# One layer of delta-rule attention and a routed feed-forward: two small TensorE products change places with the projections beside them

## The reference, cut to what matters

```python
q = l2norm(silu(conv4(xn @ Wq)))      # xn = layernorm(x), k alike, v without l2norm
k = l2norm(silu(conv4(xn @ Wk)))
v = silu(conv4(xn @ Wv)); beta = sigmoid(xn @ Wb)
for each token:                       # per head, S is 64 x 64
    u = beta * (v - k @ S)
    S = S + outer(k, u)
    o = q @ S
x = x + rmsnorm(o) * norm_w @ Wo
x = x + ffn(layernorm(x))
```

## Time and profile before

| what | value |
|---|---|
| three runs | 1350.03, 1355.93, 1358.77 us, median 1355.93 |
| span of the profiled execution | 1354.5 us; its own time is not listed beside it |
| mean granted TensorE clock of that execution | 0.984 |
| PE busy over the span | 1305.2 us |
| DVE, ACT, POOL busy | 868.2, 372.6, 336.6 us |

### The profile page before, as it was taken

The page is one execution under the profiler, slowest core; times in us unless marked ns, Lnnn a source line. Parts: engine busy times, 40 slices in busy tenths (PEclk is TensorE's granted clock), DMA queues, the critical chain, the costliest instruction groups (busy, mean ns, idle before and its releaser), DMA issues.

```text
span 1354.5 us, 27271 instructions
## 1 busy us (share of the span) xinstructions
PE 1305.2 (96%) x8466; PEld 824.9 (61%) x8467; DVE 868.2 (64%) x2426; ACT 372.6 (28%) x816; POOL 336.6 (25%) x396
## 2 busy tenths in 40 slices
PE   8968999999999999999999999999999999999996
PEld 7857777887777556544444455555555555555553
DVE  4896688559667523845111477777777777777774
ACT  4745545555453223220000011111111111111111
POOL 1211214232222211313564012212222122122221
PEclk9989999999999999999999999999999999999997
DMA  4525742733456496246447555566665565664420
GB/s 158 97 45 112 109 111 68 147 96 82 98 132 156 103 238 136 81 148 219 190 179 249 174 123 109 110 173 149 134 140 130 128 138 128 129 135 74 73 50 1
DMA packets 208513, 171.05 MB, mean 126 GB/s; under 512 B 71472, under 2 KB 160560, under 8 KB 208432
## 3 DMA queue, kind: packets, MB, share of 16 engines
q1 hardware_dynamic: 135056, 114.16, 32.3%
q0 software_dynamic: 16496, 34.23, 12.8%
q10 hardware_dynamic: 56880, 21.54, 7.6%
HBM read 91.06 MB, written 82.73 MB: 128 GB/s over the span
## 4 chain that ended last, share of the span: by engine, by line
PE 53%; DVE 2%; issue 0%; POOLq 0%; DVEq 0%; ACT 0%
PE pD L2182 15%; PE pG L2162 14%; PE pU L2171 13%; PE pG L2126 3%; PE pU L2126 3%; PE pD L2145 3%; DVE ups L2072 1%; PE pU L2120 1%; PE pD L2140 0%; POOLq L1897 0%; DVE w L1784 0%; DVE w L1785 0%; DVE route_keep L1783 0%; DVE q L1803 0%; DVE qf L1796 0%
## 5 line engine op out<-in xcount | busy, mean ns | idle before, releaser
L2072 DVE STREAM_TRANSPOSE ups<-a 32x96 f32<-32x96 f32 (+1 forms) x1264 | 330.2, 261 | 42.9
L1969 POOL DMA_INDIRECT out<-y,ix x79 | 123.0, 1557 | 482.0 <-ACT y L2025 328.3
L2182 PE MATMUL pD<-w,ups 128*128 (+1 forms) x474 | 219.3, 599 | 3.6 <-DVE ups L2072 3.6
L2171 PE MATMUL pU<-w,xsT 128*128 x632 | 199.9, 459 | 0.0
L2162 PE MATMUL pG<-w,xsT 128*128 x632 | 199.9, 458 | 0.0
L2162 PEld LDWEIGHTS pG<-w,xsT 128*128 128x128 f32 x632 | 119.5, 189 | 88.4 <-issue 37.5
L2171 PEld LDWEIGHTS pU<-w,xsT 128*128 128x128 f32 x632 | 120.1, 190 | 66.9
L950 PE MATMUL pProj<-front_region 128*128 128x256 f32 x624 | 158.4, 398 | 2.0 <-ACT front_region L697 1.6
L2182 PEld LDWEIGHTS pD<-w,ups 128*128 128x128 f32 (+1 forms) x474 | 90.8, 192 | 98.0 <-issue 81.7
L1311 DVE SCALAR_TENSOR_TENSOR front_region<-front_region,cw 128x256 f32<-128x256 f32 x288 | 131.7, 498 | 14.5 <-ACT front_region L733 11.1
L950 PEld LDWEIGHTS pProj<-front_region 128*128 128x128 f32 x624 | 115.3, 194 | 21.5 <-ACT front_region L733 2.3
(11 more groups left out here) (240 smaller groups left out, 1591.8 us busy)
## 6 DMA issues: line engine op xcount, KB each, us to landing
w<-in_up_T SPq DMA_DIRECT2D x16, 1408.0 KB
slot_rows<-zeros SPq DMA_DIRECT2D x79, 266.0 KB, 6.5
xs<-slot_rows ACTq DMA_DIRECT2D x316, 64.0 KB
w<-in_down_T SPq DMA_DIRECT2D x16, 512.0 KB
front_region<-in_L_attn_hidden_states SPq DMA_DIRECT2D x16, 256.0 KB, 3.8
x2r<-in_L_attn_hidden_states SPq DMA_DIRECT2D x16, 256.0 KB, 5.0
partial_sums<-x2r SPq DMA_DIRECT2D x16, 256.0 KB, 3.6
x_normed<-x2n SPq DMA_DIRECT2D x16, 256.0 KB, 2.4
```

The lines of the kernel that those rows point to most:

```text
L1969: pool.indirect_dma_start(out=flat, out_offset=bass.IndirectOffsetOnAxis(ap=ix[1 - par][:, 0:1], axis=0), in_=y[1 - par][:, :], in_offset= ...
L2072: dve.transpose(aT[par][B * to:B * to + B, 0:n, rows], a[rows, 0:len(IC) * P].rearrange("p (c n) -> p c n", c=len(IC))[:, 0:n, B * to:B * ...
L2171: mm = pe.matmul(pU[0][:, 0:I], xsT[par][:, k, :], w[:, bass.ds(slot, 1), 2 * I * k + I:2 * I * (k + 1)], start=(k == 0), stop=(k == DC - 1))
L2182: mm = pe.matmul(pYq[:, :], aT[1 - par][0:m, c, :], down[0:m, :, UPW + D * c:UPW + D * (c + 1)], start=(c == 0), stop=(c == 2))
```

## The change

Three moves, no instruction added or taken away. On PE, `merge_x(u)` goes from behind the slot 0 projection to directly behind `hop_r`, and `scores(u + 1)` goes from ahead of the slot 1 projection to behind it, directly ahead of `hop_u`. On ACT, `x_copy(u)` goes from behind the slot 0 `raw_copy` to ahead of it.

```diff
@@ ACT, slot loop @@
                     if tile_ok(u) and s in (2, 5):
                         s_copy(u, s // 3)
                         o_copy(u, s // 3)
+                    if s == 0 and tile_ok(u) and u < FUSED:
+                        x_copy(u)
                     if even and pair_ok(pk):
                         raw_copy(3 * DC * pk + s)
...
                     if tile_ok(u) and s in (1, 4):
                         u_copy(u, s // 3)
-                    if tile_ok(u) and s == 0 and u < FUSED:
-                        x_copy(u)
@@ PE, slot loop @@
                     if tile_ok(u) and s in (2, 5):
                         hop_o(u, s // 3)
-                    if s == 1 and tile_ok(u + 1):
-                        scores(u + 1)
+                    if s == 0 and tile_ok(u):
+                        merge_x(u)
                     if even and pair_ok(pk):
                         project(3 * DC * pk + s)
                     if not even and pair_ok(pq) and not (pq == PAIRS - 1 and s >= 4):
                         project(3 * DC * pq + SLOTS + s)
                     if old == PAIRS - 1 and even and s < 2:
                         project(3 * DC * old + SLOTS + 4 + s)
+                    if s == 1 and tile_ok(u + 1):
+                        scores(u + 1)
                     if tile_ok(u) and s in (1, 4):
                         hop_u(u, s // 3)
...
                     if s == 0:
-                        if tile_ok(u):
-                            merge_x(u)
                         if u + 3 == NT - 2:
                             qT(NT - 1)
```

## The result

The changed kernel takes 1357.98 us, the kernel before 1354.34 us (medians of 20 runs each): a ratio of 1.0028 with a 95% interval of 1.0014 to 1.0041. That is 3.6 us more, small but resolved. The forecast was +4.1 us, and 1360 us in all, which is 2.0 too high; 1.6 of that comes from the starting point, a median of three runs at 1355.93.

What follows compares the result with a forecast made beforehand. PE, busy 1305.2 of 1354.5 us, was taken as the bound. Terms 1 to 3 gave 5.7 us, the clock -1.6, so +4.1 to a span of 1358.6, and with 1.4 for the median 1360 us, range 1355 to 1365.

Steps and rivals of the forecast that it cites:

- Term 1: Tiles 0 to 10: merge_x loses the projection hiding its wait on ACT's copy, and waits 0.32 to 1.06 us.
- Term 2: Slots 0 and 1: second projection starts 1.00 us after the first, waiting for ACT's bank reads, in odd tiles and 10.
- Term 3: Tiles 0 to 10: fewer changes between large and small products on PE save 0.20 us a tile.
- Absorption: Tiles 3 and 7, where DVE carries the inverse: PE's delay of 0.56 us is taken back, leaving 0.
- Term 4: Even tiles with betas: one stretch of low clock fewer, -1.6 us, bounds -4.9 and +3.3.
- slower rival: New waits around merge_x lower the clock in 11 tiles: 1374.6 us, half of it, 1366, likelier; chance 0.16.
- faster rival: Clock stays up in all even tiles and the first copy is ready in time: 1353 or 1349 us; chance 0.17.

Runs made afterwards that it cites:

- e3: Changed kernel with ACT's copy of the first merge product (w_copy) ahead of the two silus of slot 5: ratio 0.9961 to the kernel before, six runs.
- e6: Changed kernel without zero_rows in tiles 0 and 1, those stores being made later: ratio 1.0022 to the kernel before.
- e9: Changed kernel with w_copy ahead of the silus and zero_rows kept out of tiles 0 and 1: ratio 0.9989 to the kernel before.
- e11: The kernel of e3 run once more: ratio 0.9989 to the kernel before, median 1352.07 us.
- e5: Changed kernel, but tile 1 keeps the old place of merge_x on PE and x_copy on ACT: ratio 1.0005 to the kernel before.
- e8: The kernel before, unchanged, run for a second profile: one time of 1352.28 us.
- e10: The kernel before with zero_rows kept out of tiles 0 and 1, as control: ratio 0.9996 to the kernel before.
- e2: The kernel before with only the scores moved, directly ahead of hop_u: ratio 0.9985 to the kernel before.
- e1: Changed kernel with scores back at the old place, so only merge_x and x_copy moved: ratio 1.0006 to the kernel before.
- e4: Changed kernel with ACT's x_copy back behind raw_copy: ratio 1.0031 to the kernel before.
- e7: Changed kernel with w_copy ahead of the silus and tile 1 in the old order: ratio 0.9980 to the kernel before.

## Why the prediction was right, point by point

- **Term 1** (merge_x loses its cover, 5.9 us over 11 tiles) held: 6.5 us in 12 waits, of which tile 11 had 0.7 already. Tiles 5, 6 and 10 came to 0.34, 0.94 and 1.06 us between the end of hop_r and merge_x, against 0.35, 0.93 and 1.06. Tile 8 was off, 0.93 instead of 0.33: PE was late in tile 7 (half clock in its output product, shown above), so merge_w had no DMA wait, and ACT lost the head start that this wait had given it. The output product of tile 7 is at half clock in seven of the thirteen profiles, of both orders, and exactly those seven have no DMA wait in tile 8. That the queue of ACT is the cause is shown by e3: the waits fell to 1.3 us. The Trainium skill states the rule ("TensorE: Matmul & The Clock Gate", section "Architectural detail: the array is 16× 32×32, not 1× 128×128": ScalarE works strictly in order), and e3's 5.2 us agree with it.
- **Term 2** (projections wait for ACT's reads) held: 0.40 in tiles 3, 5 and 9 and 0.84 of wait in tile 10, where the start came 1.00 us after the end. (The fifth wait of the row, in tile 0, is the old one of the earlier trace rows.) In tile 7 a transpose that waits for DVE stands between the projections and covers it. In tile 1 it shows in the profiles without a long stop (e6, e9, e11); otherwise the stop hides it.
- **Term 3** (fewer changes between small and large products) was sized too small. Beyond 0.11 for scores and 0.09 for the projection, betas between two projections take 1.70 instead of 1.88, and hop_u behind scores 1.02 or 1.03 instead of 1.07. That is 0.24 more in each of the five even tiles with betas and 0.04 in the others, about 1.4 us. So tiles 0 and 2 grew by 0.20 and 0.48 us, not by 0.45 and 0.73, and tiles 5, 9 and 10 by 0.50, 0.51 and 1.69, not by 0.56, 0.56 and 1.86. Hop_r beside merge_x couldn't be seen to gain: merge_x waits there.
- **Absorption** held in tile 7 and not in tile 3. In tile 7 the wait on the residual is 1.89 or 1.90 us in the three profiles of the old order and 1.44 or 1.45 in after, e5 and e6, and the wait of a transpose for DVE (tile vh) fell from 0.69 to 0.34: 0.8 us taken back, more than the 0.56 of the prediction. In tile 3 the residual's wait fell from 1.08 to 1.04 only, and the tile grew by 0.52 us. The missing DMA wait of tile 8 (1.2 us) is not absorption, since e8 and e10 lack it too.
- **Term 4** (clock, -1.6) came to -1.1 by the split over 20 runs, with an uncertainty of 0.8, and to -1.7 in tiles 0 to 10 of the profile (3.4 us in place of 5.1 in each of the three old ones). So its size is not known well, and its agreement with -1.6 is partly luck: the prediction had neither the stop's stretch nor that of tile 7's output product. In the profiles the stretches behind betas are all gone: 3 in the profile of before, 2 in e8, 2 in e10, 1 in e2, which all have merge_x behind its projection, and none that begins there in the nine profiles in which it stands ahead. What came in their place is the mechanism of the slower rival, on a small scale: half clock behind merge_w, hop_r, the wait and merge_x, in tile 10 (e1, e4), tile 6 (e5), tile 4 (e7, e11) and tile 8 (e3, e7, e9, e11), with some 1.6 us lost each time, and once, in e7's tile 8, some 5. In tiles 4 and 8 the long wait among them is that of merge_w for its DMA (0.9 to 1.8 us), not the new one. It did not come in each of 11 tiles, as that rival's end would have it.
- **Not in the sum**: the stop of PE in tile 1, 2.0 to 2.6 us in four profiles of the new order (0.4 in e11), with half clock behind it. It is worth 1.6 us of rest in the timed runs (e6 against after, e5 alike), which is the 1.97 us of the profile less the 0.40 of term 2 that it hides. The sum without it is 5.7 - 1.4 (term 3) + 0.6 (tile 8) = 4.9 for the waits; with it 6.5, where the split has 4.8 and the profile's tiles 5.3. The 1.2 to 1.7 us between them are not accounted for; the split's neglect of idle time at half clock may be part of it.

So the sign, the size and the main mechanism were right. That the size came so close is partly luck: two errors of more than 1 us each, a gain that was undersized and a stop that was missed, nearly cancelled. The faster rival failed as said: both waits appeared wherever the cover was missing. For the other two edits, ACT's x_copy had slack (e4), and scores behind the projection hurt nothing (e2).

## What to carry to other kernels

Before a product is moved forward on a full engine, work out when its input is ready: here the projection in between was not in the way but was the cover, and the cost could be read off to 0.01 us in tiles 5, 6 and 10 from the end of the copy in the old trace (it missed by 0.6 in tile 8, where another wait had changed). If the move is wanted, move the producer's copy ahead in its own queue first (e3: 3.6 us of rest back), and check that two users of one bank don't become neighbours. When spans of single profiles differ by as much as the effect, compare the distance between like instructions, and split the timed runs by their granted clock, but look in a trace for where half clock stands and whether PE had work there.

## What the runs showed of the hardware that had not been expected

- **PE can stop for a late packet of instructions, and full DMA engines make it late.** Ahead of the stop the DMA engines were full with stores of zeros; with these stores away, the packet began 3.5 us earlier and the stop was gone (e6, e9, e10: none in three profiles). In the ten other profiles tile 1 had a stop of 0.2 us or more in nine. All 15 stops without a releaser ended 2.4 to 3.8 us after such a packet began.
- **The stops stand at fixed places in PE's order of instructions, and that is why the new order suffers.** In tile 1 the first place is 32 matmul records behind hop_r in both orders: behind the whole merge_x in the new one (after, e1, e3, e4, e11), behind the projection's 8 and 24 of merge_x in the old one (e7, e8). The old order gets there 2.5 us after the end of hop_r (140.81 to 143.31 in e8), the new one 1.0 us after it (140.41 to 141.45), so it needs the packet 1.5 us sooner. The stops of e2, e5 and the second one of e11 share a place too, ahead of the last two records of a projection, and so do four in tile 13, behind 12 of hop_u's 16.
- **Betas, 16 matmuls of 8 columns, cost 1.88 us between small products and 1.70 between large ones.** With a projection ahead only they cost 1.77 or 1.78 (e1), with one behind only 1.81 (e2), so each side gives about half. The reason wasn't tried.
- **A half clock stretch can take as much as the wait that comes before it**: in e1's tile 10 the wait is 0.99 us, and the projection that follows takes 1.5 us longer.
